# Channel attention with the halo of keys, values and extremes carried from band to band, and three buffers for rows of exponentials

## The reference

```python
K, PAD = 7, 3
x_pad = jnp.pad(x, ((0, 0), (0, 0), (PAD, PAD), (PAD, PAD)))
q = jnp.einsum('bchw,oc->bohw', x, w_q)
kmap = jnp.einsum('bchw,oc->bohw', x_pad, w_k)
vmap = jnp.einsum('bchw,oc->bohw', x_pad, w_v)
kwin, vwin = _unfold2d(kmap, K), _unfold2d(vmap, K)      # [b, c, h, w, 7, 7]
kwin = jnp.concatenate([kwin[:, :half] + rel_h, kwin[:, half:] + rel_w], axis=1)
attn = jax.nn.softmax(q[..., None] * kwin.reshape(b, cout, h, w, K * K), axis=-1)
out = jnp.sum(attn * vwin, axis=-1)
```

## Time and profile before

| | |
|---|---|
| median of 3 runs | 8120.62 us (8116.14 to 8125.58) |
| the profiled execution | 8114.73 us, of which span 8113.0 us |
| channel attention within the span | from about 3240 to 7442 us |
| PE busy over the whole span | 7639.8 us (94%) |
| DVE, ACT, POOL busy | 5850.9 (72%), 3633.4 (45%), 4558.3 us (56%) |
| multiply, L1913 | 3136 times, 747 ns each |
| exponential, L1789 | 3136 times, 598 ns each |
| weigh, L1826 | 896 times, 3309 us busy |

### The profile page before, as it was taken

How to read it: one execution, slowest core, us unless ns; L and a number is a source line. 1 busy time by engine, 2 the same in 40 slices (tenths; PEclk the granted TensorE clock), 3 DMA queues, 4 the chain that set the end, 5 groups by cost and what they waited for, 6 DMA issues and landing times. The chain is left out here.

```text
span 8113.0 us, 142887 instructions
## 1 busy us (share of the span) xinstructions
PE 7639.8 (94%) x55554; PEld 6564.9 (81%) x55554; DVE 5850.9 (72%) x9141; ACT 3633.4 (45%) x7024; POOL 4558.3 (56%) x1996
## 2 busy tenths in 40 slices
PE   5999998899998997899999999999999999997999
PEld 4777776789997775688888888888888888886999
DVE  5666665344443554999898988999898988996664
ACT  3556565333332332445555454545555455544222
POOL 3555551033331000578778787878877787876232
PEclk9999999999998998999999999999999999998999
DMA  3111114855558773000000000000000000002452
GB/s 143 57 67 58 59 60 154 279 142 144 144 148 232 206 198 92 8 19 9 16 19 13 11 14 19 15 18 11 13 19 14 11 13 19 16 9 74 149 162 81
DMA packets 616222, 595.11 MB, mean 73 GB/s; under 512 B 464085, under 2 KB 481621, under 8 KB 610374
## 3 DMA queue, kind: packets, MB, share of 16 engines
q1 hardware_dynamic: 581318, 483.44, 21.3%
q0 software_dynamic: 33856, 96.69, 3.3%
q10 hardware_dynamic: 576, 8.39, 0.3%
HBM read 394.64 MB, written 193.76 MB: 73 GB/s over the span
## 5 line engine op out<-in xcount | busy, mean ns | idle before, releaser
L1826 POOL TENSOR_TENSOR e_ev<-e_se,e_v 128x2048 f32<-128x2048 f32 (+1 forms) x896 | 3308.9, 3714 | 898.5 <-ACT e_se L1789 893.5
L1789 ACT ACTIVATE e_se<-e_stage 128x512 f32<-128x512 f32 x3136 | 1869.7, 598 | 2041.6 <-PE e_stage L1656 1996.2
L1913 DVE SCALAR_TENSOR_TENSOR e_stage<-e_k,e_rl,e_qp 128x512 f32<-128x512 f32 x3136 | 2307.8, 747 | 301.4 <-ACT e_se L1789 262.8
L1663 PE MATMUL e_pe_sum<-e_ident,e_se 128*128 128x128 f32 x12544 | 1877.0, 272 | 12.4 <-ACT e_se L1789 12.2
L1663 PE MATMUL e_pv_sum<-e_ident,e_ev 128*128 128x128 f32 x12544 | 1869.4, 272 | 0.4 <-POOL e_ev L1826 0.4
L1663 PEld LDWEIGHTS e_pe_sum<-e_ident,e_se 128*128 128x128 f32 x12544 | 1555.7, 140 | 240.9 <-ACT e_se L1789 16.8
L1663 PEld LDWEIGHTS e_pv_sum<-e_ident,e_ev 128*128 128x128 f32 x12544 | 1483.9, 141 | 226.9 <-issue 174.5
L1656 PE MATMUL e_stage<-e_top,e_minus 128*128 128x512 f32 x3136 | 1507.2, 481 | 51.2 <-DVE e_stage L1913 46.6
L911 POOL DMA_DIRECT2D agg<-c_ot x384 | 334.8, 874 | 878.5 <-ACT c_ot L989 768.9
L403 POOL TENSOR_TENSOR a_pr<-a_pr,a_rden 128x480 f32<-128x480 f32 x512 | 495.0, 988 | 543.9 <-DVE a_rden L636 543.9
L1656 PEld LDWEIGHTS e_stage<-e_top,e_minus 128*128 128x128 f32 x3136 | 595.0, 190 | 111.0 <-DVE e_stage L1913 81.1
(11 more groups left out here) (170 smaller groups left out, 11454.2 us busy)
## 6 DMA issues: line engine op xcount, KB each, us to landing
qkv<-b_ot SPq DMA_DIRECT2D x120, 512.0 KB, 5.9
c_xt<-qkv SPq DMA_DIRECT2D x384, 160.0 KB, 3.8
agg<-c_ot POOLq DMA_DIRECT2D x384, 160.0 KB, 2.5
f_ws<-in_L_w_sets SPq DMA_DIRECT2D x32, 1152.0 KB, 8.0
a_xb<-in_x SPq DMA_DIRECT2D x24, 768.0 KB, 5.1
a_xr<-in_x SPq DMA_DIRECT2D x32, 512.0 KB, 3.8
x<-a_xr SPq DMA_DIRECT2D x32, 512.0 KB, 2.7
b_xc<-x SPq DMA_DIRECT2D x32, 512.0 KB, 6.1
```

What stands on the lines that cost most here:

```text
L1663: last = nc.tensor.matmul(acc[:, c * PART:(c + 1) * PART], lhsT=src[:, c * PART:(c + 1) * PART], rhs=ident[:], is_transpose=True, start=j ...
L1789: nc.scalar.activation(se[(t * K2 + o) % NSE][:, i], stage[:, bank_of(t, j), :], ACT.Exp)\
L1826: nc.gpsimd.tensor_tensor(split(ev[(t * NG2 + g) % NEV][:, 0:size]), split(se[(t * K2 + o) % NSE][:, i:i + size]), window(v[h], h, u, o, i ...
L1913: nc.vector.scalar_tensor_tensor(rows(stage[:, bank_of(t, j), :]), win, rl[:, h, o:o + 1], rows(qp[:]), ALU.add, ALU.mult).then_inc(multip ...
```

## The change

Only the rows of keys and values that the band before did not have are projected. Each band of an image but the first takes the six rows that it shares (`HALO`) from its own buffer of the band before, moved by a DMA inside SBUF that ACT's queue issues (`carry_keys`, `carry_values`); `carry_near` and `carry_pairs` do the same for the extremes. A first band of an image ("opens") gets zeros by DMA and three more rows by projection (K0, V0). Pieces are now whole rows of 64 columns: K1, K2, V1, V2 of 8 rows = 512 columns, K0 and V0 of 3 rows = 192 columns. `PROJ_AT` and `NEAR` change to match; `pair` and `near` become one tensor each with both extremes. In even halves a new step (the edge step, a `tensor_scalar` from `k` to `pair`) stands ahead of each pair step, since the pair step no longer covers the padded columns. POOL clears `xb`, both `k`, both `v`, `near` and `pair` at the start. `NSE` is 3.

```diff
-CLEARED = {"a": 2, "e": 3, "f": 6}
+CLEARED = {"a": 2, "e": 9, "f": 12}
...
-        NSE, NEV, NST = 4, 4, 3
+        NSE, NEV, NST = 3, 4, 3
...
-        PROJ_AT = ({0: 0, 7: 1, 14: 2, 24: 3, 30: 4, 33: 5}, {0: 6, 2: 7, 4: 8, 6: 9})
+        HALO = K2 - 1
+        NH2 = NB * HALVES
+        FRESH, WAS = HALO, R2
+        PROJ_AT = ({0: "K0", 7: "K1", 14: "K2", 24: "Q1", 29: "Q2"}, {2: "V0", 6: "V1", 12: "V2"})
+        ROWS_OF = {"0": (PAD, PAD), "1": (FRESH, RT), "2": (FRESH + RT, RT)}
...
-        NEAR = [(4, 0, 0, 0), (6, 0, 1, 0), (8, 0, 0, 1), (10, 0, 0, 2), (11, 1, 0, 0), (13, 1, 1, 0),
-                (14, 0, 1, 1), (15, 0, 1, 2), (16, 1, 0, 1), (17, 1, 0, 2), (18, 2, 0, 0), (19, 2, 1, 0),
-                (20, 1, 1, 1), (21, 1, 1, 2), (22, 2, 0, 1), (24, 2, 0, 2), (25, 2, 1, 1), (26, 2, 1, 2),
-                (28, 3, 0, 0), (29, 3, 1, 0), (30, 3, 0, 1), (31, 3, 0, 2), (32, 3, 1, 1), (33, 3, 1, 2)]
+        KEYS_AT, VALUES_AT, NEAR_AT = 1, 18, 3
+        PIECES = ((0, 3), (3, 3), (6, 2))
+        NEAR_FIRST = [(4, "K0", 0, 0), (6, "K0", 1, 0), (8, "K0", 0, 1), (10, "K0", 1, 1)]
+        NEAR = [(11, "K1", 0, 0), (13, "K1", 1, 0), (14, "K1", 0, 1), (15, "K1", 0, 2), (16, "K1", 0, 3), (17, "K1", 1, 1),
+                (18, "K2", 0, 0), (19, "K2", 1, 0), (20, "K1", 1, 2), (21, "K1", 1, 3), (22, "K2", 0, 1), (24, "K2", 0, 2),
+                (26, "K2", 0, 3), (28, "K2", 1, 1), (29, "K2", 1, 2), (30, "K2", 1, 3)]
...
+            def carry_keys(H):
+
+                act.wait_ge(multiplied, (2 * H - 2) * NTAP)
+                to = k[H % 2]
+                if opens(H):
+                    act.dma_start(to[:, 0:PAD * PW], zeros[:, 0:PAD * PW]).then_inc(keys_carried, 16)
                 else:
+                    act.dma_start(to[:, 0:HALO * PW], to[:, WAS * PW:(WAS + HALO) * PW]).then_inc(keys_carried, 16)
...
+            def carry_near(H):
+
+                act.wait_ge(ext_step, exts(H - 2, NEXT_))
+                if opens(H):
+                    act.dma_start(near[:, :, 0:PAD * PW], zeros.rearrange("p (i n) -> p i n", i=2)).then_inc(near_carried, 16)
+                else:
+                    act.dma_start(near[:, :, 0:HALO * PW], near[:, :, WAS * PW:(WAS + HALO) * PW]).then_inc(near_carried, 16)
...
+                if j == NEAR_AT and H % 2 == 1 and H + 1 + u < NH2:
+                    (carry_near, carry_pairs)[u](H + 1 + u)
...
-            nc.gpsimd.memset(xb[:], 0.0).then_inc(cleared, 1)
+            for x in (xb, *k, *v, near, pair):
+                nc.gpsimd.memset(x[:], 0.0).then_inc(cleared, 1)
...
+                if s == 0 and H:
+
+                    dve.wait_ge(ext_step, exts(H, 0))
+                    dve.wait_ge(near_carried, carries(H + 1))
...
+                    if h == 0:
+                        a = pair[:, i, first * PW:first * PW + 1]
+                        z = k[0][:, first * PW + 1:first * PW + 2]
+                        edge = [[PW, size], [WW + 2, 2], [1, PAD]]
+                        nc.vector.tensor_scalar(bass.AP(tensor=a.tensor, offset=a.offset, ap=[a.ap[0]] + edge),
+                                                bass.AP(tensor=z.tensor, offset=z.offset, ap=[z.ap[0]] + edge), 0.0, None, op)\
+                            .then_inc(near_step, 1)
```

More of the change, by code:

```diff
@@ L1413, in channel_attention @@
         v = [sb(f"v{u}", [PART, HPX]) for u in range(2)]
-        pair = [sb(f"pair{i}", [PART, HPX]) for i in range(2)]
-        near = [sb(f"near{i}", [PART, HPX]) for i in range(2)]
+        pair = sb("pair", [PART, 2, HPX])
+        near = sb("near", [PART, 2, HPX])
         high = sb("high", [PART, BPX])
@@ L1492, in tiles, with opens, parts, made @@
             return n * (TPB * per) + (t * per + more)
-        def halves(n, h, per, more):
-            return n * (HALVES * per) + (h * per + more)
+        def opens(H):
+            return H // HALVES % RB == 0
+        def parts(H):
+            return [p for p in ("K0", "K1", "K2", "Q1", "Q2", "V0", "V1", "V2") if opens(H) or p not in ("K0", "V0")]
+        def made(H, p=None):
+            return sum(len(parts(i)) for i in range(H)) + (parts(H).index(p) + 1 if p else 0)
+        def near_of(H):
+            return [x for x in NEAR_FIRST if x[3] == 0 or H % HALVES == 0] + NEAR if opens(H) else NEAR
+        def nears(H, p=None):
+            last = [x[1:] for x in near_of(H)].index((p, 1, 0)) + 1 if p else 0
+            return sum(near_before(i, len(near_of(i))) for i in range(H)) + near_before(H, last)
+        def near_before(H, s):
+            return sum(2 if x[3] == 0 and H % HALVES == 0 else 1 for x in near_of(H)[:s])
+        def exts(H, more):
+            return H * NEXT_ + more
+        def carries(H):
+            return 16 * (min(H, NH2 - 1) - 1)
         def window(t, h, u, o, i, taps):
@@ L1690, in back @@
                 if copies:
-                    pe.wait_ge(proj_copied, halves(n, (t + 1) // 2 + 1, NPJ, copies))
+                    pe.wait_ge(proj_copied, copies)
                 if near_:
-                    pe.wait_ge(near_step, halves(n, (t + 1) // 2 + 1, NNEAR, near_))
+                    pe.wait_ge(near_step, near_)
                 if t > 0 or n:
@@ L1726, in _ @@
                     .then_inc(stage_open, 1)
-            pe.wait_ge(minus_ready, 1)
-            for c in range(NPJ):
+            for p in parts(0):
                 for g in range(HALVES):
-                    project(0, 0, c, g)
+                    project(0, p, g)
             all_bands(step)
@@ L1802, in step @@
                     place_query(n, t + 1)
+            act.wait_ge(cleared, CLEARED["e"])
             normalise(0)
-            for c in range(NPJ):
-                copy_projection(0, 0, c)
+            for p in parts(0):
+                copy_projection(0, p)
             place_query(0, 0, first=True)
@@ L1861, in near_step_of @@
                     return
[L1862 to L1865 removed]
+                low, part = (0, size) if p == "K0" else PIECES[piece - 1]
+                away = (1, PW)[h]
+                at = (first + low) * PW if h == 0 else (first + low - HALO) * PW + PAD
+                a = pair[:, i, at:at + 1]
@@ L1874, in extreme_step @@
+                nc.vector.tensor_reduce(grid(near[:, i])[:, first + low:first + low + part, PAD:PAD + WW], pairs, AX.XY, op)\
+                    .then_inc(near_step, 1)
+            def extreme_step(H, s):
+                h = H % 2
                 if s == 0:
-                    dve.wait_ge(near_step, halves(n, h, NNEAR, NNEAR))
+                    dve.wait_ge(near_step, nears(H + 1))
                 else:
-                    dve.wait_ge(ext_step, halves(n, h, NEXT_, s))
+                    dve.wait_ge(ext_step, exts(H, s))
```

206 lines of the change are left out of this document (106 added, 100 removed).

## The result

The changed kernel takes 8,099.05 us by its median over six runs (8,087.2 to 8,102.0), the kernel before 8,118.38 in the same comparison (six runs, 8,113.8 to 8,125.6). The ratio is 0.9972, with a 95% interval of 0.9961 to 0.9984: faster by 0.28%. The forecast was 8,078, range 7,965 to 8,125. It names the right case, and it is 21 us too low: of the 43 us that it took off, 19 came.

The account below looks back on a forecast made before the run. It took PE as the bound with DVE close behind. Tile, opening and start terms summed to -129 us, plus 86 for held edge steps -43; from 8,114.7 profiled, plus 6 to the median, 8,078 us, range 7,965 to 8,125.

Parts of the forecast that it names:

- held: Main case: edge steps in even halves wait for POOL's instruction to end; 8,078 us, 50%.
- unheld: Rival case: edge steps in even halves do not wait for POOL; 7,992 us (7,965 to 8,015), 30%.
- the four waits of an even half: Edge steps of an ordinary even half: first and third free, second waits 2.0 us, fourth 3.3, sum 5.3.
- The price of the hold: Edge-step waits behind POOL: twelve ordinary even halves 64 us, three opening ones 22, together 86.
- The clock is no term below: Channel attention: granted clock 1.00, the full 2.4 GHz, so no time was booked for the clock.
- PE's work: Fewer, wider projection matmuls save 1.7 us in each key tile and each value tile.
- the waits for values: Value tiles: three PE waits for ACT's copies of values go, saving 2.7 us a tile.
- that 0.75: Value tiles: 0.75 us given back because DVE is late next, around its reciprocals at taps 3 to 9.
- Odd key tile: Key tile of an odd half: 0.9 of PE's 1.7 us lost to DVE's longer reduces, net -0.8.
- Even key tile, unheld: Key tile of an even half if nothing holds the edge steps: DVE 25.4 against PE 25.6, net -1.7 us.
- Openings: Halves opening an image: extra projections, and carries 3.1 us late in four odd ones; 18 us in all.
- Buffers, carries, start: Three exponential buffers cost nothing, ACT hides DMA issues, and the start nets +6 us: memsets +10.7, DVE steps -5.

Follow-up runs that it names:

- e1: Changed kernel with the edge step writing only one column, read from PSUM in place of SBUF: 7,997.6 us, ratio 0.9841 to the kernel before.
- e11: Kernel before plus four SBUF-to-SBUF tensor_scalars with a constant per even key tile, 48-column additions and 512-column max or min: 8,234.5 us, ratio 1.0135.
- e12: Kernel before plus four SBUF-to-SBUF tensor_scalars per even key tile that add an SBUF column, over 48 and 512 columns: 8,238.7 us, ratio 1.0140.
- e6: Kernel before with its four value parts projected at taps 0, 3, 6, 9 in place of 0, 2, 4, 6: 8,041.1 us, ratio 0.9895.
- e4: Changed kernel with four buffers of exponentials in place of three: 8,096.0 us, ratio 0.9963 to the kernel before.
- e9: Changed kernel with every carry issued as two transfers of half the size: 8,100.4 us, ratio 0.9968 to the kernel before.
- e2: Kernel before plus four 48-column SBUF-to-SBUF tensor_scalars per even key tile, into scratch that nothing reads: 8,225.2 us, ratio 1.0123.

## Why the prediction was right, and where it was off

- **The case.** Of held and unheld it took held, at 50%, and named the four waits of an even half as free, 2.0, free, 3.3. The steps are 0.19, 2.00, 0.18 and 3.38 us long. It worked out where each edge step would stand against GpSimd's pairs of instructions and read off what is left of the instruction. That the total lies in the range says less, since the range was made to hold both main cases.
- **The price of the hold: the mis-sized term.** 86 us were booked; by the even key tiles of the changed kernel and of e1 it is 12 x 5.84 + 3 x 10.18 = 101. The waits themselves were right: 5.07 us at taps 13 and 19 of an ordinary even half, where 5.3 was booked, and 7.4 in an opening one, where 7.3 was; 83 in all. But the sum stopped at VectorE and made TensorE late by the length of the wait and no more. "The clock is no term below" was read from a profile whose loop has no idle time of TensorE over 1 us and a clock of 1.00 throughout. With the waits came clocks of 0.50, and what is left of the 101, 0.8 us in an ordinary even half (mean of the nine with a fall and the three without) and 2.8 in an opening one, is some 17 us that the sum lacked. In the three tiles without a fall nothing is left: they are 5.1 us above e1's.
- **The reason for choosing held.** It leaned on a tensor_tensor of another layer against reciprocals, and called it close. The row that spoke most directly against it, the extremes' tensor_scalar, was missed by the false statement that there was none. So the choice owed something to luck. It came out right for a finer reason: e11 and e12 show that packed steps at the fast pace are held and leave that row standing.
- **PE's work and the waits for values.** -3.65 was booked for a value tile. The 24 ordinary ones show -3.98; the -3.87 of the table is the mean with seven opening ones, which have V0. e6 gives 2.8 us for the waits alone, 2.7 booked. The loss to VectorE and to the wait at tap 2, together some 0.5, was booked as 0.75, and that 0.75 does not come out of its own working: the steps named there add up to 5.0 us by the lengths given, not 4.4. The size was near, but part of it has another cause: the prediction saw only the reciprocals and not that the projection at taps 0 and 1 had covered ScalarE's copy of the sums.
- **Odd key tile.** -0.8 booked, -0.55 measured. The long reduces take 1.54 us by their lengths, 1.42 from start to start, where 1.43 was estimated.
- **Even key tile, unheld.** -1.7 booked; e1 gives 65.32 - 63.66 = 1.66.
- **Openings.** The wait for the carry at the four odd openings was booked at 3.1 us. The view of the carry's instructions shows 12.7 us over 4, first its issue of 0.64 us and then its landing in 3.0. The -0.7, +0.7 and -0.6 in the sum for the openings were given no source.

```profile
L1794 ACTq DMA_DIRECT2D e_near<-e_near x12: 636/637/708, 3321.4 to 6927.1; - x12
...
  DVE e_pair L1938: 12.7, 4
...
DMA to landing us min/median/max: 3.0/3.0/3.6
```

- **Buffers, carries, start.** Nothing, nothing and +6 booked. e4 and e9 show nothing. The start took 71.2 to 73.9 us in six profiles of kernels built on the one before and 79.1 to 81.7 in six built on the changed one: +8.4 by the medians.
- **The whole.** The sum has -43: -49 for the loop and +6 at the start. (The 6 us that it adds to the profiled run lead to the median and are no gain or loss.) Without the hold the loop was to lose 135, and e1 shows 140. The hold was to give back 86, and by the two loops it gives back 103. So the loop came to -37 and the start to +8: -30 where -43 was booked, and the clock alone is more than that difference. The medians say -19, with 13 to 32 as their interval. The other 11 us belong to no step of the sum; the stages ahead, whose code is unchanged, differ by 16 between the two profiles.

## What to carry to other kernels

Before a short VectorE step goes from SBUF to SBUF beside GpSimd work, expect it to wait out the other engine's instruction, however few columns it has, unless the trace shows that very form beside such an instruction and short. Reading one side from PSUM ended it here. When a wait of some microseconds reaches TensorE, look at the granted clock right after it, since the wait may be only part of the bill (5.1 of 5.8 us a tile here, by the mean). And when projections or other matmuls are taken out of a place, ask whose copy they had been hiding there.

## What was not expected of the hardware

- A step of 48 columns, 0.18 us by itself, took up to 4.05 us behind a GpSimd multiply of 4.2 us (e2), whatever its operation and scalar.
- A packed fp32 tensor_scalar of 512 columns took 0.42 us (constant) or 0.48 us (column) and was held in 15 of 15 meetings; one with 0.75 us, whose input is a window, in none of 124. The scalar_tensor_tensor on the same window, with two inputs from SBUF, took 0.74 to 0.75 us in all 733 cases from 3400 to 7400 us of the changed kernel, 610 of them begun under a GpSimd multiply.
- In the middle of a busy stage TensorE's granted clock fell to 0.50 after waits of a few microseconds: 12 of 15 of 3.3 us, all three of 1.92 us, none of 15 of 1.64 to 1.81 us in the changed kernel, and all 15 of 3.8 us in e2. In the tile shown it was back some 3 us after the matmuls began again.
